# Attention values taken from layer 0's router product in a fused two-layer kernel (Mamba-2 mixer and experts, then attention and experts)

## The reference, cut to what matters

```
x = L0_attn_x                                     # 8 sequences x 512 x 128, float32
mod0, mod1 = (silu(c) @ wmod) per sequence        # shift, scale, gate of both halves; gates ga, gb
h = layernorm(x) * (1 + ca) + sa
x = x + ga * (h + mamba2(h))                      # layer 0's mixer
h = layernorm(x) * (1 + cb) + sb                  # cb, sb of layer 0
logits = h @ gate_w.T                             # 8 experts, top 2, capacity 640
x = x + gb * experts0(h, logits)                  # an expert with more tokens than the capacity adds nothing
h = layernorm(x) * (1 + ca1) + sa1                # layer 1
Q, K, V = h @ Wq.T + bq, h @ Wk.T + bk, h @ Wv.T + bv
x = x + ga1 * (softmax(Q K' / 8) V @ Wo.T + bo)
h = layernorm(x) * (1 + cb1) + sb1
x = x + gb1 * layernorm(h + top-2 experts1(h)) * gamma + beta   # beta inside the norm
```

## Time and the profile before

| what | value |
|---|---|
| median of 3 runs | 578.16 us (577.39 to 578.57) |
| the profiled execution | 577.6 us, span 575.8 us |
| mean granted clock of TensorE | 0.961 |
| PE, PEld busy | 507.9 us (88%), 421.3 us (73%) |
| DVE busy | 440.7 us (77%) |
| ACT, POOL busy | 352.7 us (61%), 283.6 us (49%) |

### The profile page before, as it was taken

One profiled execution on the slowest core, in us unless ns is written; L12 is line 12 of the kernel. 1 busy time (PEld: TensorE's weight loads), 2 busy tenths in 40 slices (PEclk: granted clock), 3 DMA queues, 4 the chain that ended last, 5 costly groups with the idle time before them and its releaser, 6 DMA issues.

```text
span 575.8 us, 13591 instructions
## 1 busy us (share of the span) xinstructions
PE 507.9 (88%) x3328; PEld 421.3 (73%) x3328; DVE 440.7 (77%) x1651; ACT 352.7 (61%) x944; POOL 283.6 (49%) x349
## 2 busy tenths in 40 slices
PE   4799999999999999979999998623999999999990
PEld 3478888888888887746776766523999999989630
DVE  3858898989898989966898988873666667666275
ACT  3988787787869584553555555411656666555354
POOL 2134363535363534410266666772676766666323
PEclk9979999999999999998999999955999999999996
DMA  8299999999400000006411111112222222222293
GB/s 274 81 296 169 168 164 168 166 166 169 110 20 20 1 19 2 19 19 193 153 39 39 38 35 40 43 50 60 63 71 67 76 72 69 67 68 67 79 278 110
DMA packets 76394, 54.77 MB, mean 95 GB/s; under 512 B 10524, under 2 KB 69408, under 8 KB 76184
## 3 DMA queue, kind: packets, MB, share of 16 engines
q1 hardware_dynamic: 70352, 43.39, 39.6%
q0 software_dynamic: 4320, 8.99, 4.6%
q10 hardware_dynamic: 1640, 1.45, 0.8%
HBM read 40.62 MB, written 31.58 MB: 125 GB/s over the span
## 4 chain that ended last, share of the span: by engine, by line
PE 61%; issue 23%; ACT 5%; DVE 4%; SPq 3%; DMA 3%; DVEq 0%; ACTq 0%
PE bank L1912 12%; PE bank L1930 11%; PE bank L732 6%; PE bank L734 5%; PE bank L733 5%; PE bank L850 4%; PE bank L779 2%; PE bank L871 2%; PE bank L857 2%; PE bank L790 2%; PE bank L842 2%; SPq L1275 2%; PE bank L772 2%; PE bank L1903 1%; ACT front L1500 1%
## 5 line engine op out<-in xcount | busy, mean ns | idle before, releaser
L1369 POOL DMA_INDIRECT results<-arena x71 | 76.3, 1074 | 53.6 <-ACT arena L1465 48.9
L1327 POOL DMA_INDIRECT queue<-arena,pos x64 | 63.1, 987 | 32.7 <-DVE x L1568 14.1
L1912 PE MATMUL bank<-front,arena 128*128 128x128 f32 x568 | 77.5, 280 | 1.8 <-issue 1.2
L1930 PE MATMUL bank<-h_all,front 128*128 x568 | 75.2, 275 | 0.2 <-issue 0.2
L297 POOL TENSOR_TENSOR arena<-arena,half_neg 128x1 f32<-128x1 f32 x32 | 19.8, 617 | 109.5 <-ACT arena L486 109.5
L1912 PEld LDWEIGHTS bank<-front,arena 128*128 128x128 f32 x568 | 70.2, 194 | 4.5 <-issue 3.7
L1930 PEld LDWEIGHTS bank<-h_all,front 128*128 128x128 f32 x568 | 69.0, 192 | 0.3 <-issue 0.3
L1696 DVE COPY arena<-arena 128x516 f32 x71 | 35.2, 496 | 43.5 <-PE bank L1912 35.0
L1459 ACT ACTIVATE front<-bank 128x128 f32<-128x128 f32 x71 | 19.7, 278 | 54.7 <-PE bank L1903 40.3
L1709 DVE TENSOR_SCALAR front<-bank,arena 128x128 f32<-128x128 f32 x142 | 42.8, 343 | 4.3 <-PE bank L1912 4.0
L732 PE MATMUL bank<-h_hi,wc_hi 128*128 128x512 f32 x96 | 44.6, 465 | 1.3 <-ACT arena L465 1.3
(11 more groups left out here) (295 smaller groups left out, 1384.7 us busy)
## 6 DMA issues: line engine op xcount, KB each, us to landing
queue<-in_pad_rows SPq DMA_DIRECT2D x8, 2178.0 KB, 36.6
arena<-queue SPq DMA_DIRECT2D x71, 66.0 KB
rows<-mod_rows SPq DMA_DIRECT2D x8, 384.0 KB, 6.3
x_keep<-x SPq DMA_DIRECT2D x8, 256.0 KB, 2.0
arena<-in_w SPq DMA_DIRECT2D x1, 2048.0 KB, 9.0
h_all<-in_w SPq DMA_DIRECT2D x1, 2048.0 KB, 8.1
h_all<-results SPq DMA_DIRECT2D x8, 256.0 KB, 5.1
arena<-results SPq DMA_DIRECT2D x8, 256.0 KB, 5.3
```

The costliest lines, as they stand in the source:

```text
L1327: pool.indirect_dma_start(k.queue, bass.IndirectOffsetOnAxis(ap=pos[:, s, i, c0 + j:c0 + j + 1], axis=0), row[:, s * NC + c0 + j, i, :], N ...
L1369: pool.indirect_dma_start(k.results, bass.IndirectOffsetOnAxis(ap=xg[:, c, D:D + 1].bitcast(I32), axis=0), yw[:, c, :], None).then_inc(S[f ...
L1912: mm = t_.matmul(bank[(2 if g < NG // 2 else 6) + p][:, g * P:g * P + P], wc[:, p, g * P:g * P + P], xt[:, p, :], start=True, stop=True)
L1930: mm = t_.matmul(bank[4 + p][:, 0:D], ht[:, p, g * P:g * P + P], w2[:, e, g, :], start=(g == 0), stop=(g == NG - 1))
```

## The change

The second normed row is evicted once, unscaled, into `h_next`. The scale of layer 0's router is folded into `gw`, that of layer 1 into Wv Wo times the gate, both per sequence, in one tile `wvg` of 136 columns; PE's logits product becomes one product of 136 columns that gives values and logits. What the shifts and biases add is constant in a sequence: logits get `lgb`, x gets a row (`RES_G`) before attention, queries and keys get `bqk`; those rows go through DRAM. Queries and keys use weights scaled per sequence (`wqk`).

Slot work of the mixer:

```diff
@@ PE @@
+                if s == 1:
+                    t_.transpose(bank[7][:, 0:P], k.attn_w[:, 2, :], ident[:])
+                    t_.transpose(bank[7][:, P:2 * P], k.bv[:], ident[:]).then_inc(S["o_w"], 1)
                 if ("out", s) in seventh:
+                    wait(pe, "v_ev", evicted)
+                    if s == 2:
+                        t_.matmul(bank[7][:, P:2 * P], wvT, k.attn_w[:, 3, :], start=True, stop=True)
+                        t_.matmul(bank[7][:, 2 * P:3 * P], bvT, k.attn_w[:, 3, :], start=True, stop=True)
+                    if s == 3:
+                        t_.matmul(bank[7][0:NB, P:2 * P], mod[:, 1, 0, :], k.wvo[:], start=True, stop=True)
+                        t_.matmul(bank[7][0:NB, 2 * P:2 * P + NE], mod[:, 0, 3, :], gw[:], start=True, stop=True)
+                        for i in range(2):
+                            t_.matmul(bank[7][:, 264 + i * NB:264 + i * NB + NB], k.attn_w[:, i, :], mod[:, 1, 0, :], start=True, stop=True)
...
-                        mm = t_.matmul(bank[7][:, P:P + NE], h_all[:, t // NC, (t % NC) * P:(t % NC) * P + P], gw[:], start=True, stop=True)
+                        wait(pe, "w_fold", 2 * (t // NC + 1))
+                        mm = t_.matmul(bank[7][:, P:2 * P + NE], k.h_next[:, t // NC, (t % NC) * P:(t % NC) * P + P], k.wvg[:, (t // NC) % 2, :], start=True, stop=True)
@@ ACT @@
+            def value_leaves(s):
+                t = s - 4
+                wait(act, "o_r", seventh["out", s] + 1)
+                ac.activation(h_all[:, t // NC, (t % NC) * P:(t % NC) * P + P], bank[7][:, P:2 * P], ACT.Copy).then_inc(S["v_ev"], 1)
...
+                if chunk(s - 5):
+                    value_leaves(s - 1)
...
-                        ins = ac.activation(h_all[:, tb, at:at + P], bank[6][:, 3 * P:4 * P], ACT.Identity,
-                                            scale=mod[:, 0, 4, tb:tb + 1], bias=mod[:, 0, 3, tb:tb + 1])
-                        ins = ac.activation(k.h_next[:, tb, at:at + P], bank[6][:, 3 * P:4 * P], ACT.Identity,
-                                            scale=mod[:, 1, 1, tb:tb + 1], bias=mod[:, 1, 0, tb:tb + 1])
+                        ins = ac.activation(k.h_next[:, tb, at:at + P], bank[6][:, 3 * P:4 * P], ACT.Copy)
@@ DVE @@
+                    if s == 3:
+                        v.tensor_tensor(bias_rows[:, 0:D], bank[7][0:NB, P:2 * P], bvo[0:NB, :], ALU.add).then_inc(S["c_mod"], 1)
+                        v.tensor_copy(bias_rows[:, D:], bank[7][0:NB, 2 * P:2 * P + NE])
+                        v.tensor_scalar(k.bqk[:, 0, :], bank[7][:, 264:272], k.attn_b[:, 0:1], 0.125, ALU.add, ALU.mult)
+                        v.tensor_scalar(k.bqk[:, 1, :], bank[7][:, 272:280], k.attn_b[:, 1:2], None, ALU.add)
+                        v.tensor_tensor(bias_rows[:, 0:D], bias_rows[:, 0:D], rk[:, GA1, :], ALU.mult).then_inc(S["c_mod"], 1)
...
-                        ins = v.tensor_copy(lg[:, t, :], bank[7][:, P:P + NE])
+                        ins = v.tensor_tensor(lg[:, t, :], bank[7][:, 2 * P:2 * P + NE], k.lgb[:, t // NC, :], ALU.add)
@@ POOL: bias(b - 2) at c == 0 ahead of L297, fold(b) at c == 0 behind it (fold(0) in slot 3) @@
+            def fold(b):
+                to = k.wvg[:, b % 2, :]
+                g_.tensor_scalar(to[:, D:], gw[:], mod[:, 0, 4, b:b + 1], None, ALU.mult)
+                g_.tensor_tensor(to[:, 0:D], k.wvo[:], rows[:, b, GA1, :], ALU.mult).then_inc(S["w_fold"], 1)
+                g_.tensor_scalar(to[:, 0:D], to[:, 0:D], mod[:, 1, 1, b:b + 1], None, ALU.mult).then_inc(S["w_fold"], 1)
...
+            def bias(b):
+                pool.wait_ge(S[f"rows_in{b}"], 32)
+                pool.wait_ge(S[f"x_kept{b}"], 16)
+                wait(pool, "l2_xn", NC * (b + 1))
+                g_.tensor_tensor(x[:, at, :], x[:, at, :], over_rows(rows[:, b, RES_G, :], NC), ALU.add).then_inc(S["x_bias"], 1)
@@ SP, in place of the nine filling transfers and, behind them, the x_keep loop @@
+            sp.wait_ge(S["c_mod"], 7)
+            sp.dma_start(k.mod_rows[:, 0:D + NE], bias_rows).then_inc(S["r_out"], 16)
+            sp.wait_ge(S["r_out"], 32)
+            sp.dma_start(k.lgb[:], ...).then_inc(S["r_out"], 16)
             sp.dma_start(k.queue[NE * REGION:, :], ...)                        # 528 KB
+            for b in range(NB):
+                for e in (0, 1) if b == 0 else range(b + 1, min(b + 2, NB)):
+                    sp.dma_start(k.queue[e * REGION:(e + 1) * REGION, :], ...)     # 2178 KB each
+                wait(sp, "res_1", b + 1)
+                sp.dma_start(rows[:, b, RES_G, :], k.mod_rows[b:b + 1, 0:D].broadcast_to([P, D])).then_inc(S[f"rows_in{b}"], 16)
+                wait(sp, "o_x", NC * (b + 1))
+                sp.dma_start(k.x_keep[b], ...).then_inc(S[f"x_kept{b}"], 16)
```

Attention:

```diff
@@ DVE @@
-                if c == 1 and seq(b + 2):
-                    v.tensor_tensor(wvg[:, s % 2, :], wvo[:], k.gate_rows[:, 1, s, :], ALU.mult)
-                    v.tensor_tensor(bvg[:, s % 2, :], bvo[:], k.gate_rows[:, 1, s, :], ALU.mult).then_inc(S["v_gate"], 1)
...
-                if c == 0 and seq(b + 1):
-                    v.tensor_tensor(vv[:, s % 2], bank_of(("v", s))[:]..., over_chunks(bvg[:, s % 2, :]), ALU.add).then_inc(S["u_dve"], 1)
...
+                if m - 4 in ends_at:                  # wa, reciprocal, product: the row weights, before at m - 3
@@ PE @@
-                if c == 0 and seq(b + 1):
-                    value(b + 1)
+                if c == 0 and seq(b + 2):
+                    query(b + 2, first)
-                if c == 2 and seq(b + 2):
-                    query(b + 2, first)
-                if c == 3 and seq(b + 2):
+                if c == 2 and seq(b + 2):
                     key(b + 2)
@@ ACT @@
+                if c == 3 and seq(b + 3):
+                    ac.activation(wqk[:, s % 2], k.attn_w[:, 0:2, :], ACT.Copy, scale=mod[:, 1, 1, s:s + 1]).then_inc(S["w_qk"], 1)
```

More of the change, by code:

```diff
@@ L77, in __init__ @@
         self.bo = sb("bo", [P, D])
+        self.wvo = sb("wvo", [P, D])
+        self.wvg = sb("wvg", [P, 2, D + NE])
+        self.lgb = sb("lgb", [P, NB, NE])
+        self.bqk = sb("bqk", [P, 2, NB])
         self.br = sb("br", [P, NE])
@@ L1028, in kept_scalar @@
             if True:
+                for b in range(NB):
+                    ac.activation(h_all[:, b, :], k.h_next[:, b, :], ACT.Identity, scale=k.mod[:, 0, 4, b:b + 1], bias=k.mod[:, 0, 3, b:b + 1]).then_inc(S["g_cnt"], 1)
                 act.wait_ge(S["g_sh"], 1)
@@ L1339, in body @@
                     g.memset(row[:, :, :, D + 2:ROW], 0.0)
+                if m == 1 and first:
+                    k.bias(NB - 1)
                 for q, j in scatters_at.get(m, ()):
@@ L1853, in body @@
                     wait(pe, "o_r", k.ends["o_r"])
+                    wait(pe, "v_ev", NT)
                 if chunk(m + 1):
```

179 lines of the change are left out of this document (98 added, 81 removed).

## The result

The changed kernel is slower. Its median is 583.54 us (582.37 to 584.51, 4 runs), that of the kernel before 578.00 us (577.39 to 578.57, 4 runs, taken beside it): ratio 1.0086, 95% interval 1.0062 to 1.0110. The forecast was 574.7, and its range ended at 579.4. The profiled execution took 584.51 us, span 582.7, so span against span it is +6.9 us.

A forecast was written before the change was run, and what follows sets the result against it. PE was taken to bound the mixer, PE and DVE handing over to each other the attention. Terms 2.2 + 1.3 + 1.5 - 0.5 - 1.3 - 6.7 = -3.5 us gave 574.7 us; range 571.0 to 579.4.

The forecast's parts named there:

- The gate on POOL: Mixer, sequence 0: POOL waits 6 us at the bias for a copy, delaying DVE and PE; +1.5 us, bounds 0 and 5.
- The fold there puts L279 1.3 later ...: free, by little.: Mixer, later sequences: the fold delays L279 by 1.3 us, against 1.06 before L607 plus PE's 0.6; no cost.
- the small rival: Fold on POOL ahead of L279: free up to 1.66 us, beyond that slower, 579.9 at 2.4 us; chance 0.14.
- POOL holds DVE: Rival: 24 new POOL instructions lengthen DVE's long ones by 7.4 us, a third reaching PE, so 577.2; chance 0.06.
- Columns: Mixer: PE's logits product of 136 instead of 8 columns costs 0.09 us a chunk in 25 chunks; +2.2 us, bounds 0 and 7.4.
- ACT's -0.5: Mixer: ACT's evictions take 0.38 us less a slot, which could shorten PE's idle time; -0.5 us, 0 to -1.2.
- Early work: Mixer slots 1 to 3: two turns of additional products on a full PE; +1.3 us, bound 2.
- The transition: Mixer's end beside the first attention slots: some 2 us of PE and DVE work gone, under half counted; -1.3 us, 0 to -3.
- The attention: Attention sequences: value products, their evictions and pairs go from PE and DVE; -6.7 us, bounds -3.3 and -11.4.
- the fold's rival (579.9): Mixer: POOL's three fold instructions at 0.8 us each, 2.4 in all, delay L279 in every sequence; chance 0.14.
- the chance of 0.17 for slower: Whole kernel slower: the fold on POOL, plus attention giving only half together with the gate at its bound; 0.17.

The follow-up runs named there:

- fold_ahead: Changed kernel with the fold moved ahead of the power of the row scale (L321) in POOL's order; ratio 1.0096 to the kernel before.
- after_again: Changed kernel, unchanged, run and profiled again on another chip beside the kernel before; ratio 1.0111.
- first pair: First profiles of the kernel before and the changed kernel, the latter's execution at 584.51 us; ratio of the kernels 1.0086.
- gate_fold: Changed kernel with bias rows and copies of x issued ahead of filling transfers, and the fold ahead of POOL's power L321; ratio 0.9962 to the kernel before.
- no_pool_work: Changed kernel with every bias, and the folds from sequence 2 on, replaced by empty POOL instructions with the same waits; ratio 1.0003 to the kernel before.
- gate_free: Changed kernel with each sequence's bias row and copy of x issued ahead of the filling transfers; ratio 1.0039 to the kernel before.
- res_ahead: gate_free with POOL's first residual instruction (L330) issued ahead of the power L321; ratio 0.9996 to the kernel before.
- fold_behind: gate_free with the fold a slot later in POOL's order, behind L301 and L308; ratio 0.9961 to the kernel before.
- after: First profile of the changed kernel, without further edits; profiled execution 584.51 us, median 583.54 us.
- narrow: gate_fold with only the 8 logits columns in the mixer's product, the values' 128 left out; ratio 0.9942 to the kernel before.
- second pair: The kernel before and the changed kernel, both unchanged, profiled together on another chip; ratio 1.0111.
- bias_end: bias_later with four of the biases left to the attention's slots 1 to 4; ratio 0.9968 to the kernel before, 0.9951 when run again.
- leaves_at_end: gate_fold with ACT evicting the values of slots 28 to 33 at the end of its mixer slot; ratio 0.9962 to the kernel before.
- bias_later: Changed kernel with filling still first, the fold ahead of the power and each bias four slots later; ratio 0.9944 to the kernel before, 0.9947 again.

## Why the prediction was wrong

**The gate on POOL: the mechanism right, its size wrong.** This is the costliest step. It said that POOL would come to `bias(0)`, stand there for 6 us until about 101, and hold L279 and with it DVE and PE; measured were 5.98 us, until 101.98. That the landing came out so close is in part luck: on the other chips the copy landed at 103.9 to 105.7, 9.1 to 9.8 us after its issue. Behind that each term was too small. The bias took 1.70 where 1.28 was used (1.26 in fold_ahead and after_again; here it began 0.2 us behind a DVE instruction of 128x512, L558, which no run tests as the reason), L301 ended at 106.1 where 104.6 was expected, DVE was 3.65 late, not 1.9, and PE 2.77, not 1.3. And a term was missing: PE came back at a granted clock of 0.50, which the first pair's rows put at 1.6 us more. On other chips the wait was 8.4 and 9.0 us, PE's 4.7 and 4.8. Together it is 7.6 us between fold_ahead and gate_fold, 5.5 where only the wait is left (no_pool_work), against +1.5 with a bound of 5 in the sum. In the first pair it was less: the eight slots lost 5.2 us with the fold's share in them.

**"The fold there puts L279 1.3 later ...: free, by little."** This step failed. The rule counted only how late L279 may be for the next turn on PE. The fold took 1.4 us from its start to its end, under the 1.66 that the small rival gave as its limit, so by the text's own rule it was free; it cost 4.4 us by the ratios of gate_free and gate_fold, 3.4 by their slots. The slack was counted right: DVE waits 0.46 for L301 and PE doesn't feel it. But DVE and POOL then met in the next slot and the one after, where two tiny DVE instructions fell behind POOL's 128x512 ones and took 1.1 us instead of 0.15. res_ahead kept the fold and its wait and moved only L330, and had the later fours back at 27.3 to 27.4; fold_behind moved the fold out of the way and had all of it back.

**POOL holds DVE: the rival was right in kind.** It had 0.06 and named other instructions (24 new ones of POOL on DVE's long ones, 577.2). What it got wrong is whom it hits: not the new instructions cost most, but old ones that had passed each other by 0.8 and 0.3 us. The Trainium skill (SBUF — State Buffer, "SBUF: two separate sides") adds to the exclusive lock which DVE instructions take part: those with two inputs in SBUF or in a two-port mode. The trace agrees as far as it goes: L778 has two inputs in SBUF and is held to the end, the statistics L734 beside L330 have one and are not. L738 has one and is held; which mode it runs in, no row shows. In five profiles (after, after_again, gate_free, gate_fold, fold_behind) it went the same way each time that one of them began well inside a POOL instruction of 128x256 or 128x512: L738 was held 15 times of 15, L778 15 of 15, L612 (128x16, two inputs in SBUF) 28 of 28, and L757 (TENSOR_SCALAR of 128x1) none of 27.

**Columns: +2.2 forecast, 1.1 measured** (narrow). The product is 0.10 us longer from its start to the next one's (165.28 to 165.52 in gate_fold against 163.44 to 163.58), as taken. A part of it lies in time in which PE would have waited. With ACT's -0.5 the two were +1.7; gate_fold's full slots are 0.2 us longer than before in twenty, so in sum the two nearly cancel: narrow's twenty, without the columns, are 0.7 shorter than before, of which ACT's -0.5 is the only forecast term.

**Early work: +1.3 forecast, +0.84 and +0.97 measured.** Right in kind, 0.3 to 0.5 us too large.

**The transition: -1.3 forecast, +1.6 and +2.6 measured.** Wrong in sign. The step took "less than half" of 2 us of work saved on PE and DVE. But PE's busy time from chunk 24's power to the first update was 45.1 us before and 45.5 after in the first pair: the columns and the lower clock took what the values gave. Of the second pair's 2.6 us, 0.7 are POOL's biases where they stand (bias_end, which gave it back later), 0.2 the columns (38.08 in narrow, 38.25 in leaves_at_end), and up to 1.4 the granted clock at the end of it, which the kernel before had at 1.00 in that pair. Why the clock falls there in some executions and not in others stays open, and so does the last 0.3 us.

**The attention: -6.7 forecast, -7.5 measured in the second pair, -3.7 in the first.** The term was right where nothing disturbs it: 14.15 us a sequence to 13.07. In the first pair and on two later chips the attention has further waits, which the profile calls remote, and they were longer in the changed kernel: up to the last update 6.5 against 3.0 us on DVE in the first pair. That is as much as 3.5 of the 3.8 us between the two measurements, and 3.2 of it is the one wait before the last update of x, which was 0.5 to 3.3 us in the later profiles on such chips. What DVE waits for there isn't shown by any run.

**Against the sum.** In the second pair: early +1.0, the wait and the fold with the columns +9.8, the transition +2.6, the attention -7.5, the rest +0.5, together +6.3. With both causes taken out (gate_fold, bias_later) the ratios are 0.9962 and 0.9944, which is -2.2 and -3.2 us of 570. That this is near the -3.5 is luck: the forecast had 1.5 for the gate in it, so for these kernels it would have been -5.0, and what is missing went in the transition, where -1.3 was forecast and a loss came, while the columns and the attention came out better than forecast.

**The range.** The bound of the gate (5) and the fold's rival (579.9) were each held possible, but never together, and never with the clock; of the chance of 0.17 for slower 0.14 came from the fold, at a price that was worked out from the wrong quantity, its duration.

## What to carry to other kernels

An operation that waits for a transfer goes to where its engine has nothing urgent behind it, or a period later, as bias_later did: an engine that works in order passes the wait on to those that need it, and TensorE, which stood for 2.8 us and more here, came back at half its clock. When work is put in front of an instruction that another engine needs, slack isn't the whole test: look for short DVE instructions that pass close to long POOL ones, because here a shift of half a microsecond made them wait for nearly the whole of one. And a change that gains in one stage and loses in another needs its stages timed side by side on more than one chip; here the first pair, though both were timed side by side, showed half of what the attention gave in the second.

## What the runs showed of the hardware

- A DVE instruction of 128x4 (L738, L778) took 1.05 to 1.12 us in place of 0.15 each time it began 0.2 us behind a POOL instruction of 128x512 (after, after_again, gate_free), 1.30 where it began 0.01 behind (fold_behind, at 29.26), and 0.44 behind one of 128x256 (res_ahead), ending within 0.03 us of it each time.
- When PE had stood for 2.8 us and went on, its granted clock was 0.50 for some 3.4 us (after); when it had stood for 4.7 and 4.8, for 4.9 and 5.7 us (after_again, fold_ahead). A 512-column matmul took 0.63 us there (0.40 at full clock).
- A copy of x issued behind 4,884 KB of filling landed 7.7, 9.1, 9.5 and 9.8 us after its issue (issued at 94.12 in the first profile, 95.40 in after_again, 94.37 in fold_ahead, 95.89 in no_pool_work), the shortest of the same kernels' eight copies 2.0 us.
- The attention of the kernel before took 105.9 or 111.5 us by chip, the changed one's 98.4 or 107.8, with the granted clock at 0.99 to 1.00 and the same work. The kernels with its attention took 98.3 to 99.7 us on three chips and 106.4 to 108.9 on two others.
